# Attention and an eight-expert layer on one Trainium2 core: first expert's weights loaded in groups 24 to 30, scatters spread anew, older rows summed in the scores' banks, expert rows weighed with the bias in one step

## What is computed

```python
def _L0_attn_ref(x, W_qkv, W_out, s):        # x: 4 x 512 x 256, float32
    proj = x @ W_qkv                         # 32 query heads, 8 key/value heads, head size 64
    q, k = _apply_rope(q, cos, sin), _apply_rope(k, cos, sin)
    attn = jnp.where(mask, -jnp.inf, q k^T * sm_scale)
    w = softmax(concat([attn, sink]))[..., :-1]
    return (w v) @ W_out
def _L0_ffn_ref(x, gating_w, w1, b1, w2, b2):  # 2048 tokens, 8 experts, top 2, capacity 640
    topk_w, topk_idx = top_k(softmax(x_flat @ gating_w), 2)
    buf[e, slot] = x_flat[token]             # slot: how many tokens chose e before this one
    h = maximum(buf @ w1 + b1, 0)
    out_e = h @ w2 + b2
    out_flat[token] += out_e[slot] * weight
x = x + _L0_attn_ref(_layernorm(x), ...)
x = x + _L0_ffn_ref(_layernorm(x), ...)
```

## Time and profile before

| what | us |
|---|---|
| median of three runs (1080.97 to 1083.25) | 1081.03 |
| the profiled execution's own time | 1088.03 |
| its span, first to last instruction | 1086.2 |
| PE busy in it | 1042.8 |
| DVE busy | 874.8 |
| ACT busy | 657.7 |
| POOL busy | 708.7 |

### The profile page before, as it was taken

How to read it: one execution, slowest core, us unless ns; L and a number is a source line. 1 busy time by engine, 2 the same in 40 slices (tenths; PEclk the granted TensorE clock), 3 DMA queues, 4 the chain that set the end, 5 groups by cost and what they waited for, 6 DMA issues and landing times.

```text
span 1086.2 us, 32862 instructions
## 1 busy us (share of the span) xinstructions
PE 1042.8 (96%) x13323; PEld 753.0 (69%) x13323; DVE 874.8 (81%) x1938; ACT 657.7 (61%) x1666; POOL 708.7 (65%) x587
## 2 busy tenths in 40 slices
PE   7899999999999999999999999999888999999995
PEld 4465666666665666666666566666558999999995
DVE  7999999999899998998998899899856455555441
ACT  4666667666666666667765666777634555554441
POOL 5657866676667786776688776676742555555662
PEclk9999999999999999999999999999998999999998
DMA  4654545533333333333333334333524244444321
GB/s 113 156 133 117 141 125 141 121 96 104 79 78 91 98 111 99 97 79 88 92 89 100 97 102 109 78 78 88 150 73 166 69 117 123 123 123 122 91 51 21
DMA packets 115544, 112.13 MB, mean 103 GB/s; under 512 B 35233, under 2 KB 103905, under 8 KB 115265
## 3 DMA queue, kind: packets, MB, share of 16 engines
q1 hardware_dynamic: 97648, 90.29, 30.4%
q0 software_dynamic: 7296, 8.55, 4.8%
q10 hardware_dynamic: 10448, 11.20, 3.7%
HBM read 74.84 MB, written 21.83 MB: 89 GB/s over the span
## 4 chain that ended last, share of the span: by engine, by line
PE 58%; DVE 32%; issue 4%; POOL 2%; SPq 1%; ACT 1%; DMA 1%; POOLq 0%; another core or an unknown queue 0%; DVEq 0%
PE bank L1441 18%; DVE probs_ring L1060 14%; DVE probs_t L1069 12%; PE bank L1615 11%; PE bank L1628 10%; PE bank L1420 10%; DVE heads_sb L1089 3%; PE bank L1473 2%; PE bank L1379 1%; PE bank L1362 1%; PE bank L1593 1%; PE bank L1562 1%; PE bank L1397 1%; SPq L474 1%; ACT probs_ring L801 1%
## 5 line engine op out<-in xcount | busy, mean ns | idle before, releaser
L801 ACT ACTIVATE probs_ring<-probs_ring,neg_max 128x512 f32<-128x512 f32 x512 | 365.8, 717 | 222.4 <-DVE neg_max L1060 219.8
L1060 DVE CUSTOM_DVE_ANT_0 probs_ring<-bank,mask,sink_neg 128x512 f32<-128x512 f32 x512 | 360.1, 736 | 31.9 <-PE bank L1420 28.9
L1069 DVE STREAM_TRANSPOSE probs_t<-probs_ring 128x1024 f32<-128x1024 f32 x256 | 317.4, 1240 | 0.3 <-ACT probs_ring L801 0.2
L1420 PE MATMUL bank<-qk_st 64*128 64x512 f32 x1024 | 281.0, 625 | 17.0 <-DVE neg_max L1060 11.8
L1441 PE MATMUL bank<-probs_t,v_quads 32*64 32x256 f32 x8192 | 249.4, 382 | 1.4 <-issue 0.8
L1441 PEld LDWEIGHTS bank<-probs_t,v_quads 32*64 32x64 f32 x8192 | 180.0, 132 | 78.7 <-issue 51.0
L655 POOL TENSOR_TENSOR chunk_sb<-chunk_sb,rope_sb 128x512 f32<-128x512 f32 (+1 forms) x94 | 119.8, 1275 | 140.7 <-issue 112.1
L1420 PEld LDWEIGHTS bank<-qk_st 64*128 64x128 f32 x1024 | 85.3, 186 | 83.2 <-DVE neg_max L1060 46.0
L660 POOL TENSOR_TENSOR qk_st<-chunk_sb,swap_sb 128x512 f32<-128x512 f32 (+1 forms) x94 | 120.3, 1280 | 7.4
L1473 PEld LDWEIGHTS bank<-wo_sb,heads_sb 64*128 64x128 f32 x992 | 96.1, 187 | 37.4 <-issue 29.2
L656 POOL TENSOR_TENSOR swap_sb<-swap_sb,rope_sb 128x512 f32<-128x512 f32 (+1 forms) x94 | 120.2, 1279 | 0.0
(11 more groups left out here) (175 smaller groups left out, 1501.2 us busy)
## 6 DMA issues: line engine op xcount, KB each, us to landing
v_quads<-v_rows SPq DMA_DIRECT2D x128, 128.0 KB
recip_wide<-recip_rows SPq DMA_DIRECT2D x64, 256.0 KB
w_raw<-in_L_ffn_w SPq DMA_DIRECT2D x14, 1024.0 KB, 9.6
swap_sb<-chunk_sb SPq DMA_DIRECT2D x314, 32.0 KB, 2.6
w_raw<-in_L_attn_W_qkv SPq DMA_DIRECT2D x32, 256.0 KB, 3.0
slots<-slot_rows SPq DMA_DIRECT2D x9, 662.5 KB, 4.0
slot_rows<-x2T ACTq DMA_DIRECT2D x8, 662.5 KB, 6.1
w_raw<-in_L_attn_W_qkv SPq DMA_DIRECT2D x64, 64.0 KB, 2.7
```

The source lines that it names most:

```text
L801: nc.scalar.activation(probs[(g * UNITS + n) % RING][:, :], probs[(g * UNITS + n) % RING][:, :], ACT.Exp, bias=neg_max[j][:, n:n + 1], sca ...
L1060: nc.vector.tensor_tensor_reduce(probs[(g * UNITS + n) % RING][:, :], SCORE[SCORE_OF[n // 2][n % 2]][:, :], mask[:, L - P - t * P:2 * L - ...
L1069: nc.vector.transpose(probs_t[j][:, :, (h // 2) * (2 * P):(h // 2 + 1) * (2 * P)] .rearrange("p b (h q) -> p h b q", h=2)[:, :, :, t * BLK ...
L1420: nc.tensor.matmul(SCORE[SCORE_OF[n // 2][hh]][:, :], qk_st[j][half, h // 2, t * P:(t + 1) * P], qk_st[j][half, PAIRS, :], start=True, sto ...
```

## The change

- Loads: the first expert's w1 is loaded in two halves at step 9 of groups 24 and 25, w2 in two halves at step 13 of group 29 and step 9 of group 30; `w1_raw` and `w2_raw` lie elsewhere in SBUF. Their splits of the low parts on POOL come two steps earlier.
- Scatters: one of the three at step 9 of the seventh and eighth group moves to step 3 of the same group, and every scatter of the first three batches waits for `s_recip_in`, that is until the inverses of the group before have come back. The normalisations are three steps later.
- `old_rows` runs before the last group's probabilities times values, in the banks of the scores, instead of two `keep_warm` matmuls; these stand in front of the first expert.
- Last batch: ACT makes `last_hi` one tile ahead; two gate operations of DVE come behind the selections; the last eight products go bank by bank, so that bank 0 is done first, and `to_hidden(0)` waits for the low parts one at a time.
- Rows out: ACT writes bias times weight into `expert_sb` beforehand, DVE adds the product of PE's rows and the weight in one instruction, and POOL waits for that. POOL's wait for all additions at the end is gone (SP still has its own).

```diff
-        W1_IN_AT, W2_IN_AT = LAST - 3, LAST - 1
+        W1_IN_AT = {LAST - 7 * UNITS + 9: 0, LAST - 6 * UNITS + 9: 1}
+        W2_IN_AT = {LAST - UNITS - 3: 0, LAST - UNITS + 9: 1}
-        W1_LO_AT, W2_LO_AT = LAST + 9, LAST + 10
+        W1_LO_AT, W2_LO_AT = LAST + 7, LAST + 8
-        NORM2_AT, GATE_EXP_AT = {84: 0, 85: 1, 87: 2, 88: 3}, {71: (0, 1), 73: (2, 3)}
+        NORM2_AT, GATE_EXP_AT = {87: 0, 88: 1, 90: 2, 91: 3}, {71: (0, 1), 73: (2, 3)}
-        SCATTER_AT = {89: (0, 1), 105: (2, 3, 4), 121: (5, 6, 7)}
+        SCATTER_AT = {89: (0, 1), 99: (2,), 105: (3, 4), 115: (5,), 121: (6, 7)}
...
+        def slot_bank(e, c):
+
+            return SCORE[c] if e == 0 else banks[c]
...
                 for c in SCATTER_AT.get(r, ()):
+                    if not last:
+                        pool.wait_ge(s_recip_in, ((b + 1) * NKV + r // UNITS) * 32)
...
-                    pool.wait_ge(s_weighted, e * SLOTT + s + 1)
+                    pool.wait_ge(s_expert_sb, e * SLOTT + s + 1)
...
             add_rows(E - 1)
-            pool.wait_ge(s_added, E * SLOTT * 16)
...
-            def weigh(e):
+            def weigh_bias(e):
                 if e == 0:
+                    act.wait_ge(s_b2_in, 16)
                     act.wait_ge(s_slots_in[0], 16)
+                else:
+                    act.wait_ge(s_added, e * SLOTT * 16)
                 for s in range(SLOTT):
-                    act.wait_ge(s_expert_sb, e * SLOTT + s + 1)
-                    nc.scalar.activation(expert_sb[:, s, :], expert_sb[:, s, :], ACT.Copy,
+                    nc.scalar.activation(expert_sb[:, s, :], b2_sb[:, e, :], ACT.Copy,
                                          scale=slots[e % 2][:, s, D + 1 + e:D + 2 + e]).then_inc(s_weighted, 1)
...
             def rows_out(e):
-                if later(e):
-                    dve.wait_ge(s_added, e * SLOTT * 16)
-                else:
-                    dve.wait_ge(s_b2_in, 16)
                 for s in range(SLOTT):
+                    dve.wait_ge(s_weighted, e * SLOTT + s + 1)
                     dve.wait_ge(s_expert, e * SLOTT + (s + 1))
-                    nc.vector.tensor_tensor(expert_sb[:, s, :], FFN2[s][:, 0:D],
-                                            b2_sb[:, e, :], ALU.add).then_inc(s_expert_sb, 1)
+                    nc.vector.scalar_tensor_tensor(expert_sb[:, s, :], FFN2[s][:, 0:D],
+                                                   slots[e % 2][:, s, D + 1 + e:D + 2 + e], expert_sb[:, s, :],
+                                                   ALU.mult, ALU.add).then_inc(s_expert_sb, 1)
...
                     if PV_AT[n][0] == 0 and g == GROUPS - 1:
                         pe.wait_ge(s_chunk_out, GROUPS * CHUNKS)
-                        keep_warm(2, PROJ, x_sb[:, 0:2, :])
                         pe.wait_ge(s_b1_in, 16)
                         nc.tensor.transpose(PROJ[:, 0:E * HC], b1_rows[:, :],
                                             identity[0:E * HC, 0:E * HC]).then_inc(s_b1_turned, 1)
+                        pe.wait_ge(s_old_in, 16)
+                        for bank in (2, 1, 0):
+                            pe.wait_ge(s_neg_max, GROUPS * UNITS - bank)
+                            old_rows(bank)
...
-                if r == LOGITS_AT + 1 and last:
-                    pe.wait_ge(s_old_in, 16)
-                    pe.wait_ge(s_residual, 2 * GROUPS)
-                    old_rows(0)
-                    old_rows(1)
                 if r == SELECT_AT and last:
-                    pe.wait_ge(s_centred, B)
-                    old_rows(2)
...
+                    for i in range(len(SLOT_PIECES)):
+                        for t in (2, 3):
+                            pe.wait_ge(s_last_lo, t + 1)
+                            ins = last_rows(t, 1, i, t == 3 and i != 1)
+                        if i != 1:
+                            ins.then_inc(s_slots_turned, 1)
...
+                            if n == 0:
+                                pe.wait_ge(s_slots_lo, half + kc + 1)
...
             pe.wait_ge(s_b1, 1)
+            keep_warm(2, PROJ, x_sb[:, 0:2, :])
             for e in range(E):
```

More of the change, by code:

```diff
@@ L936, in norm2, with high_row @@
                                      bias=norm_bias[:, t:t + 1], scale=rstd[:, t:t + 1]).then_inc(s_norm2, 1)
+            def high_row(b, t):
+                nc.scalar.activation(last_hi[:, t, :], x_sb[:, b * TPB + t, :], ACT.Identity,
+                                     bias=norm_bias[:, t:t + 1], scale=rstd[:, t:t + 1]).then_inc(s_last_hi, 1)
             def act_route(r, b, last):
@@ L961, in act_route @@
                 if r == WEIGHTS_AT and last:
+                    act.wait_ge(s_rstd, b + 1)
+                    high_row(b, 0)
                     for t in range(TPB):
+                        if t + 1 < TPB:
+                            high_row(b, t + 1)
                         norm2(b, t)
[L964 to L965 removed]
                     act.wait_ge(s_neg_top, b + 1)
@@ L1204, in dve_route @@
                         step(ins)
-                        step(nc.vector.tensor_tensor(gates[:, :, :], logits[:, :, :],
-                                                     rstd[:, 0:TPB].unsqueeze(2).broadcast_to([P, TPB, E]), ALU.mult))
-                        ins = nc.vector.tensor_tensor(gates[:, :, :], gates[:, :, :],
-                                                      neg_top[:, :].unsqueeze(2).broadcast_to([P, TPB, E]), ALU.add)
-                    ins.then_inc(s_neg_top, 1)
+                    else:
+                        ins.then_inc(s_neg_top, 1)
                 if r == PLACE_AT:
@@ L1229, in dve_route @@
                                                     ALU.is_equal).then_inc(s_select, 1)
+                        if t == TPB - 1:
+                            step(nc.vector.tensor_tensor(gates[:, :, :], logits[:, :, :],
+                                                         rstd[:, 0:TPB].unsqueeze(2).broadcast_to([P, TPB, E]), ALU.mult))
+                            nc.vector.tensor_tensor(gates[:, :, :], gates[:, :, :],
+                                                    neg_top[:, :].unsqueeze(2).broadcast_to([P, TPB, E]),
+                                                    ALU.add).then_inc(s_neg_top, 1)
                         if t > 0:
@@ L1404, in keep_warm, with slot_cols, old_rows @@
                     nc.tensor.matmul(bank[:, :], identity[:, :], with_rows, start=True, stop=True)
+            def slot_cols(kc, s0, s1):
+                m = kc * SLOTT + s0
+                return slot_bank(0, m // 4)[:, m % 4 * P:(m % 4 + s1 - s0) * P]
+            def old_rows(bank):
+                nc.tensor.matmul(slot_bank(0, bank)[:, :], ones_r[:, :], before_r[:, 0:1].broadcast_to([P, 512]),
+                                 start=True, stop=False)
+                for m in range(bank * 4, min(bank * 4 + 4, KC * SLOTT)):
+                    kc, s = divmod(m, SLOTT)
+                    nc.tensor.matmul(slot_cols(kc, s, s + 1), slots[0][:, s, kc * P:(kc + 1) * P], identity[:, :],
+                                     start=False, stop=False)
             def pe_step(n, g, j):
@@ L1536, in pe_route @@
                             pe.wait_ge(s_last_lo, t + 1)
-                        last_rows(t, part)
+                        for i in range(len(SLOT_PIECES)):
+                            last_rows(t, part, i)
+                    for i in range(len(SLOT_PIECES)):
+                        for t in (2, 3):
[3 more added lines that the diff above has]
+                            ins.then_inc(s_slots_turned, 1)
                 if r in TURN_X_AT:
@@ L1601, in to_hidden @@
             def to_hidden(e):
-                pe.wait_ge(s_slots_lo, e * 3 + 3)
+                if later(e):
+                    pe.wait_ge(s_slots_lo, e * 3 + 3)
                 pe.wait_ge(s_w1_lo, e + 1)
```

61 lines of the change are left out of this document (25 added, 36 removed).

## The result

The changed kernel is slower: 1085.75 us (median of 7 runs, 1084.07 to 1090.9) against 1080.97 (7 runs, 1078.56 to 1083.25), ratio 1.0053, 95% interval 1.0031 to 1.0075. Two later comparisons on other chips gave 1.0019 (1.0000 to 1.0037, so the loss is only just told from none) and 1.0033 (1.0010 to 1.0057). Forecast were 7.3 us less; measured are 0.8 to 4.8 more. It is a difference of two starts in one trace, and so leaves out what happens elsewhere in an execution. It varies by itself, too: four traces with the attention of before have 47.19, 43.60, 43.74 and 43.05 us.

A forecast was written before the change was run, and what follows sets the result against it. PE and DVE alone were taken to set the time: DVE in ordinary attention groups, PE behind them. Terms -2.0 - 3.0 + 1.5 - 0.9 + 1.7 - 1.8 - 0.5 - 2.35 = -7.3 us gave 1073.7 us, range 1069.0 to 1080.5.

The forecast's parts named there:

- Step 3: Old rows ahead of the last block: the block starts 1.5 us later, upper bound 5.5.
- Step 2: Groups 29 to 31: without the 1 MB loads and one scatter of three, 3.0 us gained, at most 4.5.
- Step 1: Turns to groups 16 and 24: moving one scatter of three to step 3 gains 2.0 us, bounds 0 and 3.0.
- Step 4: Last batch's counts, no longer behind old rows and two gate operations: 0.9 us gained.
- Step 5: Last batch: idle PE brings a half-clock stretch onto last_rows, 1.7 us lost.
- Step 6: Start of the first expert: two keep_warm fill PE's gap and hold the clock, 1.8 us gained.
- named as a rival: PE stays at half clock through the last batch's end: 5.7 us on top, 1079.4; chance 0.12.
- Steps 7 and 8: End of kernel: 0.5 us gained in writing rows out, 2.35 us by removing POOL's last wait.
- the DRAIN keeps its old end: Rival on POOL's last wait: DRAIN ends as before, only 0.5 us won at the end, 1076.0; chance 0.06.
- The third: Rival: moved scatters stall PE's blocks at six places, 2.76 us each, making the kernel slower; chance 0.12.

The follow-up runs named there:

- e3: The change with low parts back behind the scatters and no wait for s_recip_in in group 31; ratio to before 0.9934.
- g3: As e3, with old_rows back between logits and counts and keep_warm ahead of the last block as before; ratio to before 0.9910.
- f3: The kernel before with only the scatters spread anew and their wait for s_recip_in; ratio to before 1.0020.
- g1: As f3, but without the wait for s_recip_in in group 31; ratio to before 0.9936.
- f2: The kernel before with only POOL's last wait (for s_added) taken out; ratio to before 0.9980.
- g4: The kernel before with only w1_low and w2_low moved ahead of the three scatters; ratio to before 0.9975.
- g2: The kernel before with only the first expert's weights loaded in four halves in groups 24 to 30; ratio to before 0.9977.
- f1: As e3, with two keep_warm matmuls added ahead of the last batch's counts; ratio to before 0.9934.
- h1: g3 with six of the last batch's eight scatters left out, and SP waiting for six fewer; ratio to before 0.9914.
- h2: g3 run again unchanged, beside the change on the same chip; ratio to before 0.9941, median 1075.67 us.
- e1: The change with the low parts of the first expert's weights back behind the scatters; ratio to before 0.9947.
- e4: The change with old_rows back in its old place between logits and counts of the last batch; ratio to before 0.9951.

## Why the prediction was wrong, by its steps

**Step 3 failed, and it carries the miss.** It costed `old_rows` ahead of the last block by PE's work alone, 1.5 us with an upper bound of 5.5, and never asked when `slots[0]` is loaded. In the change that load is on the path. The trace of before would have shown it: there the load lands at 796.5, 7.7 us before the place where `old_rows` now wants it, and the change puts 9.1 us of low parts and 5.3 us of waiting ahead of the last scatter, on which the load depends. Step 2 had seen both the scatters and the moved low parts, and said "what is late next" only for the inverses and value rows. From heads 30 to 31 the change takes 27.18 us and e3, with both delays away, 17.90. The difference is the 6.56 us of waiting, and `old_rows` itself, which takes 5.7 us at mostly half clock behind that wait and 3.1 in e3. Early `old_rows` without the wait costs 0.4 us (17.90 against 17.46 in g3), so the 1.5 was not too low for its own part. The 3.95 us in it, for ten small and three large matmuls, were too many by 0.9: the row's 0.61 us hold the end of the last matmul, and the steps between them are shorter. From heads 29 to 31 three kernels with the attention of before took 43.60, 43.74 and 43.05 us (mean 43.5), the change 52.9: 9.4 lost, or 8.5 if the profile of before (47.19) counts as the fourth.

**Step 1 had the right sign and missed the price of its wait.** At the two turns that it costed, to groups 16 and 24, the gain is 1.0 us, forecast 2.0 (48.7 in the mean of four traces with the old scatters, 47.7 in thirteen with the new). Groups 14, 15, 21, 22 and 23, each from the heads of the group before to its own, take 121.9 us with the old scatters (120.5 to 122.8) and 119.4 with the new (118.8 to 120.1): 2.5. The pause at a turn that step 1 read off comes in some executions only: heads 22 to 23 take 25.03, 24.60, 23.92 and 23.53 us with the old scatters. And step 1 took POOL's 5.18 us of idle time at one turn as cover for the wait for `s_recip_in` everywhere. In group 31 there is no such cover, and f3 against g1 shows 5.7 us for the wait alone.

**Step 2's 3.0 us can't be found in the traces.** Its 29.73 us came from one profiled execution that stood 7 us above the median. Three other traces with the old scatters, f2, g4 (both with the old loads) and g2, have 25.80, 25.59 and 26.27, and the change itself has 26.27, 25.80 and 23.28. Its first link is real, since the inverses' first leg is 4 us shorter with the new loads, but g2 is no shorter for it than f2. In this interval fourteen of the seventeen traces have a block longer than its usual 2.41 or 2.85 us, with either loads and either scatters; what makes them is open. The prediction said of the 7 us that they apply "to both kernels alike"; here part of them lay in the very interval from which a gain was drawn. Whether the loads remove a pause that comes now and then stays open; g2's ratio can't tell (see g4).

**Steps 4 to 6** gave -1.0 together, and hold about. Step 4: DVE takes up the counts 11.20 us behind the heads of group 31, before 12.12, 0.9 as forecast. Step 5: `last_rows` takes 7.3 us for 5.4, which is 1.9 against the 1.7 forecast; in the second trace of the change it takes 8.2. Step 6: the first expert starts 1.15 us behind the end of `last_rows`, before 2.04, and has no half clock, its period 30.33 instead of 31.36. Heads 31 to the second expert: -0.9 in these two profiles (50.99 against 51.94), -0.3 between the means of the three traces of the change (50.99, 53.84 and 51.22) and of six with the last batch of before (51.94 to 52.56). That filling the wait keeps the clock is shown by f1 and g3. The price of the idle time here is 2.6 us (e3's 21.39 less g3's 18.78). The rule of the Trainium skill that was named as a rival ("TensorE: Matmul & The Clock Gate", Part 1: the slow clock is the default, and activity lifts it) agrees with these traces.

**Steps 7 and 8 were right.** Last matmul to end of span: 11.9, 9.5 without the wait (2.4 gained, forecast 2.35), 9.1 with the rows weighed in one step (0.4, forecast 0.5). The 2.4 is read from one trace of f2; its ratio of 0.9980 alone would not tell it from nothing. DVE's instruction takes 0.48 us, the one it replaces 0.42. The Trainium skill's sentence on the recorded end ("Perfetto Trace Analysis", "DMA Instruction — SWDGE (GPSIMD)") agrees with the kernel before, where POOL's wait for the landing ended 2.2 us after it. What was drawn from it, that the DRAIN keeps its old end, is refuted: it ends 5.9 us after POOL's last indirect DMA when begun early, 8.3 before.

**The sum with measured terms:** -2.5 + 9.4 - 0.9 - 0.4 - 2.4 = +3.2 us; with 8.5 and -0.3 for the second and third term it is +2.9. Both are within the 0.8 to 4.8 of the three comparisons. None of the rivals was this one. The third had the right sign and a wrong mechanism: g1, with the moved scatters, has no long block in five of the six groups, and in the sixth some such as stand there with the old scatters too. One slip is in the chances: by the shares that the text gives the rivals, faster is 0.74 and same 0.15, not 0.76 and 0.13.

## What to carry to other kernels

When a step is moved ahead of a wait, follow what it consumes back through every queue to the last instruction that produces it, and look at what else the change puts in front of that one; here two edits on POOL, one harmless in itself (g4) and one a gain but for its wait in group 31 (g1, f3), met a third on PE. Before a gain is read off one long interval, compare it with the same interval of another execution: a profile that stands above the median has its excess somewhere, and likely in the most conspicuous place. And work that sits in a wait of PE may be what holds the clock: take it away only with something else in its place.

## What the runs showed of the hardware

- POOL's closing DRAIN lasts until 5.9 us after its last indirect DMA's recorded end when it starts at once (7.72 us, in eleven traces; 7.23 us and 5.5 after it in h1), and 5.94 us from the end of the wait when it waits for the landing (five traces).
- A 16 KB store of SP, issued beside a 1 MB load of ACT, landed after 5.1 to 5.8 us in five traces, and after 1.4 us in twelve where no such load ran.
- Among the first expert's relus (the activation behind each hidden tile) ACT pauses although the trace shows nothing that it still waits for ("remote" or PE's name in the row), up to 4.6 us, in twelve of the seventeen traces (not in before, in two of the change, in h1 and h2):

```profile
844.03 1.78 ACT L1005 ACTIVATE hidden<-bank,b_sb 128x320 f32<-128x320 f32 x4 [4.59 <-remote]
```

This row is of e1; its first expert took 33.65 us. An earlier start of that expert was partly given back in this way in e1 to e4, f1 and g3 (32.42 to 34.81 us for the period, 30.33 and 30.53 in two traces of the change and 32.24 in the third; f1 has 2.17 us of waiting for the second expert's `slots` in it). The cause is open.
